# Both maxima of a pair of heads ahead of one joint exponent bias, in a blocked attention layer

## The chip, the cores and the metric

The kernel runs on one core of a Trainium2 chip. The metric is the device time of one execution in microseconds, the median of three runs. The engines are TensorE (PE; PEld is its weight load), VectorE (DVE), ScalarE (ACT), GpSimd (POOL) and SyncE (SP), which issues the DMAs.

## What is computed

x is 4 x 1024 x 1024 (batch, tokens, features). The layer is an attention block with a conditioned norm, followed by a causal depthwise convolution of four taps. Cut to what matters here:

```python
xn = rms_norm(x, g_norm) * (1 + scale) + shift      # scale, shift from cond @ W_emb + b_emb
q, k, v = split(xn @ W_qkv)                         # 16 heads of 64
q, k = rms_norm(q, g_q), rms_norm(k, g_k)
attn = softmax(q @ k.T * 64 ** -0.5)                # per head, 1024 x 1024
o = attn @ v
x = x + o + o @ W_out
out = x + causal_conv(x, cond) + b                  # taps from cond, four rows
```

The convolution's weights are the 4 x 1024 conditioning array, one row per tap. The softmax subtracts each row's maximum. A row is one query of one head; its maximum over 1024 keys is what the change is about.

## The kernel before, in words

**Units.** There are U = 32 units (4 batches x 8 pairs of heads, K = 8). Unit u does the attention of one pair of heads for all 1024 queries, in eight steps p = 0 to 7 of 128 queries each. So there are 256 steps, and each handles both heads h = 0, 1: slot s = 2p + h. Beside its attention a unit carries, spread by hand over its eight steps, the projection of unit u + 1 (`project`, L1016), head norms (`sums`, `normalise`), the input norm of x for the next batch (`x_multiply`, `x_shift`), and from unit 8 on the output product of the batch before (`out_product`, L1050) and its convolution (`convolve`, L1703 to L1714). Float32 accuracy comes from pairs of float16 halves, high and low, so most products are three matmuls.

**One step, engine by engine.** Each engine has its own program in a fixed order, and semaphores tie them.

- TensorE: `score(u, p)` (L958) waits until both exponents of step p - 1 are done (`exp_done` at slot 2p), since there is one PSUM tile `scores` [128, 2, 1024] for both heads. It issues 12 matmuls, the two heads alternating, so that both heads' scores are complete within the last two. Then come second halves of `attend` (L977), `inverses` (L992), `project` or `out_product`, first halves of `attend`, and the next `score`. How much lies between two scores differs by p: at p = 6 and 7 of a steady unit it is least.
- VectorE: `maximum(u, p, h)` (L1558) for h = 0 and 1: a tensor_reduce over 1024 scores gives minus the row maximum, and a tensor_scalar (L1561) turns it into the exponent's bias. After both come the unit's other vector work of that step, then `low(u, p, 0)` and `low(u, p, 1)` (L1567), which wait for the high halves, then in some steps more work (`x_multiply` at p = 0, `sums` at p = 3, `normalise` at p = 5).
- ScalarE: other work, then `exponent(u, p, 0)` and `(u, p, 1)` (L1201), each waiting for `bias_done` of its own slot; each also reads out the row sum. Then `read_inverses` at even p, `high(u, p, 0)` and `(u, p, 1)` (L1209, the float16 high half), and more.
- SyncE: `transpose_p` (L762) transposes each slot's probabilities by DMA once `lo_done` tells of its low half; `attend` reads them one or two steps later.

The exponent's input stays in PSUM, in `scores`, until it has run; `prob` (in the tile `late`) has one place for each of the two heads.

**Special units.** Units 1 to 6 also prepare a part of the projection of the unit after next (`gives_early`), units 1 to 7 prepare W_out (`wo_maximum`, `wo_lower`), and unit 31 is followed by a tail of output products. `keep_clock` issues matmuls whose result nobody reads.

Of the kernel before, what the change touches and what calls it, by code (L numbers as in the profile page):

```python
# [12 lines left out]
ALU = mybir.AluOpType  # L13
ACT = mybir.ActivationFunctionType
AX = mybir.AxisListType
# [9 lines left out]
P_SHIFT = 12 * float(np.log(2.0))  # L25
# [441 lines left out]
def main(nc, const, shared, w_dram, mod_dram, xn_dram, o_dram, x, W_qkv, W_out, out):  # L467
# [15 lines left out]
    with ExitStack() as ctx:  # L483
        def sb(name, shape, dt):
            return ctx.enter_context(nc.sbuf_tensor(name, shape, dt))

        def psum(name, shape, dt):
            return ctx.enter_context(nc.psum_tensor(name, shape, dt))

        def sem(name):  # L490
            return ctx.enter_context(nc.semaphore(name))
# [18 lines left out]
        neg = sb("neg", [P, NS], F32)  # L510
        bias = sb("bias", [P, NS], F32)
# [16 lines left out]
        scores = psum("scores", [P, 2, N], F32)  # L528
# [51 lines left out]
        qk_done = sem("qk_done")  # L580
        max_done = sem("max_done")
        bias_done = sem("bias_done")
# [107 lines left out]
        def slot(u, s):  # L690
            return NS * u + s

        def static(u):
            return isinstance(u, int)
# [856 lines left out]

        @block.vector
        def _(dve):
            def maximum(u, p, h):
                s = 2 * p + h
                n = slot(u, s)
                dve.wait_ge(qk_done, n + 1)
                nc.vector.tensor_reduce(neg[:, s:s + 1], scores[:, h, :], axis=AX.X, op=ALU.max,  # L1558
                                        negate=True).then_inc(max_done, 1)
                dve.wait_ge(max_done, n + 1)  # L1560
                nc.vector.tensor_scalar(bias[:, s:s + 1], neg[:, s:s + 1], const["l_scale"][:, 0:1], P_SHIFT,  # L1561
                                        ALU.mult, ALU.add).then_inc(bias_done, 1)

            def low(u, p, h):
                s = 2 * p + h
# [29 lines left out]
            def x_mean(v, i, ring):  # L1595
                dve.wait_ge(x_sq, v - K + 1)
                need(dve, x_pw, v - K - ring + 1)
                nc.vector.tensor_scalar(msx[:, i, 1:2], msx[:, i, 0:1], 1.0 / D, EPS, ALU.mult,
                                        ALU.add).then_inc(x_ms, 1)
# [13 lines left out]
            def x_shift(v, buffer):  # L1613
                dve.wait_ge(x_mul, v + 1)
                nc.vector.tensor_tensor(buffer, buffer, rows[:, 1], ALU.add).then_inc(x_mod, 1)
# [15 lines left out]
            def wo_maxima():  # L1631
                dve.wait_ge(wo_mx, K)
                nc.vector.tensor_reduce(wo_top[:, 0:1], wo_max[:], axis=AX.X, op=ALU.max).then_inc(wo_rows, 1)
# [29 lines left out]
            def invert(u, g, par):  # L1663
                n = NG * u + g
                dve.wait_ge(exp_done, slot(u, 4 * g) + 4)
                need(dve, inv_tr, n - 1)
                col = par * NS + 4 * g
                nc.vector.reciprocal(inv[:, g % 2, :], total[:, col:col + 4]).then_inc(inv_rc, 1)
                dve.wait_ge(inv_rc, n + 1)
                one_ = inv[:, g % 2, :].rearrange("p (a h) -> p a h", a=2)  # L1670
                nc.vector.tensor_scalar(inv_pair[:, g % 2, :, 0:2], one_, INV_UP, None, ALU.mult).then_inc(inv_hi, 1)
                dve.wait_ge(inv_hi, n + 1)
                nc.vector.scalar_tensor_tensor(out=inv_pair[:, g % 2, :, 2:4], in0=one_, scalar=INV_UP,
                                               in1=inv_pair[:, g % 2, :, 0:2], op0=ALU.mult,
                                               op1=ALU.subtract).then_inc(inv_done, 1)
# [15 lines left out]
            def convolve(T, par, hh, i):  # L1691
                n = 4 * T + 2 * hh + i
                m = 2 * hh + i
                c = 4 * par + m
                y_, acc_ = yT_of(T), acc_of(T)
                if T == U - 1 and m == 2:
                    dve.wait_ge(y_first, 1)
                else:
                    dve.wait_ge(y_ev, 2 * T + hh + 1)
                if T != U - K - 1:  # L1700
                    need(dve, *stored(T - (2 if static(T) and T >= U - K else 1), hh))
                need(dve, halo, 2 * n)
                nc.vector.tensor_scalar(y_[:, m, 0:H], ends[:, c, :], const["carry"][:, bass.ds(T, 1)], None,  # L1703
                                        ALU.mult).then_inc(halo, 1)
                for k in range(TAPS - 1, -1, -1):
                    if k == TAPS - 1:
                        nc.vector.tensor_scalar(acc_[:, m, :], y_[:, m, k:k + QG], const["taps"][:, k, c:c + 1],
                                                const["conv_b"][:, c:c + 1], ALU.mult, ALU.add).then_inc(cv, 1)
                        dve.wait_ge(halo, 2 * n + 1)
                        nc.vector.tensor_copy(ends[:, c, :], y_[:, m, QG:QG + H]).then_inc(halo, 1)  # L1710
                        dve.wait_ge(halo, 2 * n + 2)
                    else:
                        dve.wait_ge(cv, 4 * n + TAPS - 1 - k)
                        nc.vector.scalar_tensor_tensor(out=acc_[:, m, :], in0=y_[:, m, k:k + QG],  # L1714
                                                       scalar=const["taps"][:, k, c:c + 1], in1=acc_[:, m, :],
                                                       op0=ALU.mult, op1=ALU.add).then_inc(cv, 1)

            def unit(u, par, qkv, xs, outs, fins):
                w, v, T = u + 1, u + K, u - K
                begun = not (static(u) and u == 0)  # L1720
                last = u + 1 == U
                for p in range(K):
                    maximum(u, p, 0)
                    maximum(u, p, 1)
                    if p == 0:
                        if xs:
                            x_mean(v, par, 2)
                        if begun:
                            invert(u - 1, 3, 1 - par)
                    if p == 1:  # L1730
                        if fins:
                            convolve(T - 1, 1 - par, 0, 1)
                        if xs:
                            x_shift(v, x_in[:])
                    if p in (2, 4, 6):
                        invert(u, p // 2 - 1, par)
                    if p == 2:
                        if outs and par == 0:
                            set_scale(T)
                        if fins:  # L1740
                            convolve(T - 1, 1 - par, 1, 0)
                    if p == 3 and fins:
                        convolve(T - 1, 1 - par, 1, 1)
                    if p == 4 and qkv:
                        normalise(w, 0)
                    if p == 5 and qkv:
                        sums(w, 1)
                    if p == 6 and qkv and not outs:
                        normalise(w, 1)
                    if last and p == 5:  # L1750
                        set_scale(U - K)
                    if u in (1, 2) and p < 4:
                        wo_maximum(4 * u - 4 + p)
                    if u == 3 and p == 0:
                        wo_maxima()
                    if u == 3 and p == 2:
                        wo_scales()
                    if 4 <= u < K and p in (2, 4):
                        wo_lower(2 * u - 8 + p // 2 - 1)
                    if p == 7 and outs and not last:  # L1760
                        convolve(T, par, 0, 0)
                    elif p == 7 and qkv:
                        read_keys(w, 1 - par)
                    if p % 2 == 0 and p >= 4:
                        scale_values(u, (p - 4) // 2)
                    elif p % 2 == 0 and begun:
                        scale_values(u - 1, 2 + p // 2)
                    low(u, p, 0)
                    low(u, p, 1)
                    if p == 0 and xs:  # L1770
                        x_multiply(v, par, x_in[:])
                    if p == 3 and qkv:
                        sums(w, 0)
                    if p == 5 and qkv and outs:
                        normalise(w, 1)
# [89 lines left out]
```

## Time and profile before

| | us |
|---|---|
| median of 3 runs | 2477.79 |
| lowest and highest | 2477.67, 2483.67 |
| span of the profiled execution | 2476.2 |
| TensorE busy | 2362.7 |
| VectorE busy | 2089.6 |
| ScalarE busy | 1825.8 |
| GpSimd busy | 641.1 |

The profile is one execution of the program; its span runs from the first to the last instruction, and the device time of a run lies 1 to 2 us above such a span. Times are in us from the start of the span. Engines overlap, so busy times don't add up. Matmuls are pipelined, and their ends are modelled. In a timeline row the number behind the start is how long the row's instructions took together, xN how many there are, and brackets give the engine's idle time ahead of them and who ended it. In a chain of waits each step is followed back to what released it.

### The profile page before, as it was taken

Reading aid. Unit: us, or ns where it says so; the run is one execution under the profiler, and the core shown is the slowest. Engines: PE = TensorE matmul, PEld = TensorE weight load, DVE = VectorE, ACT = ScalarE, POOL = GpSimd, SP = SyncE. Lnnn points to the kernel's source line nnn. Section 1 sums busy time; section 2 is a strip of 40 time slices with the busy share of each in tenths; the row PEclk is TensorE's granted clock in tenths of the full one; section 3 lists DMA queues with packets and bytes.
Section 4 is the critical chain, followed back from the end, with each engine's and each line's share of the span. In section 5 each row is a group of like instructions: output and inputs, shape, how many; then the busy total and the mean of one; then the engine's idle time right before and its main releaser. Section 6 shows DMA issues by size and latency. Waiting matters only on the chain.

```text
span 2476.2 us, 54245 instructions
## 1 busy us (share of the span) xinstructions
PE 2362.7 (95%) x20794; PEld 1524.8 (62%) x20794; DVE 2089.6 (84%) x3368; ACT 1825.8 (74%) x2834; POOL 641.1 (26%) x451
## 2 busy tenths in 40 slices
PE   4799998999899999999999999999999999999899
PEld 0455555555466666666666666666666666666688
DVE  7769888888778888888888888888888888888876
ACT  5477778888777777877777787777777777777732
POOL 1132232332233222333332223233212222221100
PEclk9899999999999999999999999999999999999999
DMA  9999999999998989999999999999988888889971
GB/s 360 311 217 223 192 183 194 180 193 224 201 196 181 197 182 213 181 199 223 201 213 182 210 186 196 184 191 228 202 174 170 180 172 163 171 166 173 182 188 52
DMA packets 1234737, 484.99 MB, mean 196 GB/s; under 512 B 1139632, under 2 KB 1197872, under 8 KB 1232048
## 3 DMA queue, kind: packets, MB, share of 16 engines
q1 hardware_dynamic: 1234480, 481.53, 92.4%
q8 instruction: 166, 2.72, 0.5%
q14 instruction: 91, 0.75, 0.1%
HBM read 137.20 MB, written 56.66 MB: 78 GB/s over the span
## 4 chain that ended last, share of the span: by engine, by line
PE 64%; DVE 20%; issue 5%; ACT 4%; SPq 2%; DMA 1%; POOL 0%; ACTq 0%; POOLq 0%
PE proj L1016 33%; PE scores L958 10%; DVE neg L1558 9%; PE values L977 9%; PE proj L1050 8%; DVE p_pair L1567 7%; ACT p_pair L1209 3%; DVE bias L1561 2%; PE proj L1056 1%; PE misc L1068 1%; SPq L762 1%; ACT late L1201 1%; DMA w_sb<-w_dram 1%; PE values L992 1%; PE values L984 1%
## 5 line engine op out<-in xcount | busy, mean ns | idle before, releaser
L1016 PE MATMUL proj<-w_sb,xn_sb 128*128 128x384 f16 x6144 | 1035.2, 327 | 20.8 <-DMA w_sb<-w_dram 13.2
L1201 ACT ACTIVATE late<-scores,bias,l_scale 128x1024 f32<-128x1024 f32 x512 | 615.6, 1203 | 344.9 <-DVE bias L1561 325.8
L1016 PEld LDWEIGHTS proj<-w_sb,xn_sb 128*128 128x128 f16 x6144 | 587.2, 98 | 425.4 <-issue 25.9
L1567 DVE TENSOR_TENSOR p_pair<-late,p_pair 128x1024 f16<-128x1024 f32 x512 | 616.2, 1245 | 124.9 <-ACT p_pair L1209 124.8
L1558 DVE TENSOR_REDUCE neg<-scores 128x1 f32<-128x1024 f32 x512 | 623.0, 1217 | 107.0 <-PE scores L958 103.6
L1209 ACT ACTIVATE p_pair<-late 128x1024 f16<-128x1024 f32 x512 | 510.9, 1050 | 0.0
L977 PE MATMUL values<-pT,v_pair 128*64 128x256 f16 x6144 | 389.7, 277 | 14.6 <-ACT inv_row L1269 14.6
L958 PE MATMUL scores<-late 64*128 64x512 f16 x3072 | 376.1, 378 | 15.0 <-ACT late L1201 12.9
L977 PEld LDWEIGHTS values<-pT,v_pair 128*64 128x64 f16 x6144 | 319.0, 111 | 94.1 <-issue 70.3
L1474 POOL TENSOR_TENSOR rs<-ms,power 128x16 f32<-128x16 f32 x63 | 183.1, 2906 | 404.1 <-DVE ms L1581 403.7
L1050 PE MATMUL proj<-late,wo 128*128 128x256 f16 x2304 | 267.7, 273 | 1.3 <-issue 1.3
L1503 POOL TENSOR_TENSOR oT_pair<-oT,oT_pair 128x256 f16<-128x256 f32 x124 | 144.4, 1164 | 461.0 <-ACT oT_pair L1285 461.0
L958 PEld LDWEIGHTS scores<-late 64*128 64x128 f16 x3072 | 128.9, 94 | 195.7 <-issue 45.6
L1050 PEld LDWEIGHTS proj<-late,wo 128*128 128x128 f16 x2304 | 220.5, 98 | 31.5 <-issue 1.6
L1479 POOL TENSOR_TENSOR qk_pair<-stage,qk_pair 128x512 f16<-128x512 f32 x126 | 145.4, 1174 | 330.4 <-ACT qk_pair L1232 330.4
L1714 DVE SCALAR_TENSOR_TENSOR late<-late,taps 128x256 f32<-128x256 f32 x324 | 157.1, 485 | 11.6
L1217 ACT ACTIVATE stage<-proj 128x384 f32<-128x384 f32 x256 | 122.2, 477 | 29.8 <-PE proj L1016 29.8
L1269 ACT ACTIVATE inv_row<-values 4x256 f16<-4x256 f16 x128 | 46.9, 366 | 119.2 <-PE values L992 119.2
L1561 DVE TENSOR_SCALAR bias<-neg,l_scale 128x1 f32<-128x1 f32 x512 | 109.7, 214 | 18.1
L1499 POOL TENSOR_TENSOR pair<-x_in,pair 128x1024 f16<-128x1024 f32 x24 | 66.2, 2757 | 206.5 <-ACT pair L1263 199.5
L1201 ACT ACTIVATION_READ_ACCUMULATOR late<-scores,bias,l_scale 128x1 f32 x512 | 98.5, 192 | 0.0
L1050 PE MATMUL proj<-xn_sb,wo 128*128 128x256 f16 x744 | 86.5, 273 | 1.2 <-ACT late L1307 1.2
(183 smaller groups left out, 2023.6 us busy)
## 6 DMA issues: line engine op xcount, KB each, us to landing
w_sb<-w_dram SPq DMA_DIRECT2D x121, 384.0 KB, 4.1
o_dram<-oT_pair SPq DMA_DIRECT2D x124, 128.0 KB, 2.4
out<-late SPq DMA_DIRECT2D x54, 256.0 KB, 2.9
x_in<-in_x SPq DMA_DIRECT2D x25, 512.0 KB, 4.6
late<-in_x SPq DMA_DIRECT2D x25, 512.0 KB, 4.1
wq_raw<-in_L_cond_W_qkv SPq DMA_DIRECT2D x8, 1536.0 KB, 11.2
late<-o_dram SPq DMA_DIRECT2D x12, 1024.0 KB, 6.1
xn_dram<-late SPq DMA_DIRECT2D x21, 512.0 KB, 3.6
```

Source lines behind the costliest of these rows:

```text
L958: last = nc.tensor.matmul(scores[:, h, n * HN:(n + 1) * HN], stack[rows_, par, i, p * P:(p + 1) * P], stack[rows_, par, j, n * HN:(n + 1) ...
L977: last = nc.tensor.matmul(values[DH * h:DH * h + DH, 0:QG].rearrange("p (a n) -> p a n", a=2), v_pair[:, par, 2 * c + h, DH * i:DH * i + D ...
L1016: last = nc.tensor.matmul(proj[:, t % 2, 0:6 * DH], xn_sb[:, t, i * K + c, :], w_sb[:, c, j, :], start=(c == 0 and i == j == 0), stop=(c = ...
L1050: last = nc.tensor.matmul(dst, const["wo"][:, c, b, m * P:(m + 1) * P], oT_[:, c, a, :], start=(c == 0 and a == b == 0 and c1 == K), stop= ...
L1201: nc.scalar.activation(prob[:, h, :], scores[:, h, :], ACT.Exp, bias=bias[:, s:s + 1], scale=const["l_scale"][:, 0:1], accum_out=total[:, ...
L1209: nc.scalar.activation(p_pair[:, s % 4, 0, :], prob[:, h, :], ACT.Copy).then_inc(hi_done, 1)
L1474: nc.gpsimd.tensor_tensor(rs[:], ms[:], const["power"][:, 0:4 * KH], ALU.pow).then_inc(h_pw, 1)
L1479: last = nc.gpsimd.tensor_tensor(qk_pair[:, j, 1].rearrange("p t (h d) -> p (t h) d", d=DH), stage[:, hf, :, j * DH:(j + 1) * DH], qk_pair ...
L1558: nc.vector.tensor_reduce(neg[:, s:s + 1], scores[:, h, :], axis=AX.X, op=ALU.max, negate=True).then_inc(max_done, 1)
L1561: nc.vector.tensor_scalar(bias[:, s:s + 1], neg[:, s:s + 1], const["l_scale"][:, 0:1], P_SHIFT, ALU.mult, ALU.add).then_inc(bias_done, 1)
L1567: nc.vector.tensor_tensor(p_pair[:, s % 4, 1, :], prob[:, h, :], p_pair[:, s % 4, 0, :], ALU.subtract).then_inc(lo_done, 1)
L1714: nc.vector.scalar_tensor_tensor(out=acc_[:, m, :], in0=y_[:, m, k:k + QG], scalar=const["taps"][:, k, c:c + 1], in1=acc_[:, m, :], op0=AL ...
```

## The change

`maximum(u, p, h)`, called for h = 0 and then h = 1, becomes `maxima(u, p)`. It issues both tensor_reduces, each behind the wait for its own head's scores, then waits for both and makes the two biases with one tensor_scalar over two columns, which raises `bias_done` by two. Nothing on the other engines changes: `exponent` still waits for its own slot's count.

```diff
--- before.py
+++ after.py
@@ -1551,15 +1551,16 @@
 
         @block.vector
         def _(dve):
-            def maximum(u, p, h):
-                s = 2 * p + h
-                n = slot(u, s)
-                dve.wait_ge(qk_done, n + 1)
-                nc.vector.tensor_reduce(neg[:, s:s + 1], scores[:, h, :], axis=AX.X, op=ALU.max,
-                                        negate=True).then_inc(max_done, 1)
-                dve.wait_ge(max_done, n + 1)
-                nc.vector.tensor_scalar(bias[:, s:s + 1], neg[:, s:s + 1], const["l_scale"][:, 0:1], P_SHIFT,
-                                        ALU.mult, ALU.add).then_inc(bias_done, 1)
+            def maxima(u, p):
+                n = slot(u, 2 * p)
+                for h in range(2):
+                    s = 2 * p + h
+                    dve.wait_ge(qk_done, n + h + 1)
+                    nc.vector.tensor_reduce(neg[:, s:s + 1], scores[:, h, :], axis=AX.X, op=ALU.max,
+                                            negate=True).then_inc(max_done, 1)
+                dve.wait_ge(max_done, n + 2)
+                nc.vector.tensor_scalar(bias[:, 2 * p:2 * p + 2], neg[:, 2 * p:2 * p + 2], const["l_scale"][:, 0:1],
+                                        P_SHIFT, ALU.mult, ALU.add).then_inc(bias_done, 2)
 
             def low(u, p, h):
                 s = 2 * p + h
@@ -1720,8 +1721,7 @@
                 begun = not (static(u) and u == 0)
                 last = u + 1 == U
                 for p in range(K):
-                    maximum(u, p, 0)
-                    maximum(u, p, 1)
+                    maxima(u, p)
                     if p == 0:
                         if xs:
                             x_mean(v, par, 2)
```

## Rows read from the trace of the kernel before

**Rows 1.** The page, busy time, share of the span and instructions of each engine.

```profile
PE 2362.7 (95%) x20794; PEld 1524.8 (62%) x20794; DVE 2089.6 (84%) x3368; ACT 1825.8 (74%) x2834; POOL 641.1 (26%) x451
```

**Rows 2.** The page, the chain that ended last, shares by engine.

```profile
PE 64%; DVE 20%; issue 5%; ACT 4%; SPq 2%; DMA 1%; POOL 0%; ACTq 0%; POOLq 0%
```

**Rows 3.** Stretches: start:end, length, busy (instructions) by engine, granted clock, DMA share, GB/s.

```profile
core 0: us, PE busy (x) PEld busy (x) DVE busy (x) ACT busy (x) POOL busy (x), PEclk, DMA share, GB/s
398.50:594.90 196.40, 182.00 (x1576) 107.54 (x1576) 167.61 (x236) 163.73 (x254) 60.27 (x42) 0.97 0.97 195
...
664.60:2308.20 1643.60, 1642.21 (x14806) 1077.15 (x14804) 1415.29 (x2261) 1266.06 (x1988) 454.92 (x308) 1.00 0.94 190
2308.20:2361.80 53.60, 44.03 (x455) 31.82 (x455) 45.54 (x79) 37.75 (x59) 3.92 (x3) 1.00 1.02 197
```

**Rows 4.** Waits over the whole span: us in total, times, longest us.

```profile
ACT late L1201 <- DVE bias L1561: 325.8, 216, 6.9
...
DVE p_pair L1567 <- ACT p_pair L1209: 124.8, 172, 2.3
```

**Rows 5.** Timeline of VectorE, from unit 15's p = 7 to unit 16's p = 5.

```profile
1231.78 1.22 DVE L1558 TENSOR_REDUCE neg<-scores 128x1 f32<-128x1024 f32 x1
1233.03 0.21 DVE L1561 TENSOR_SCALAR bias<-neg,l_scale 128x1 f32<-128x1 f32 x1
1233.16 1.21 DVE L1558 TENSOR_REDUCE neg<-scores 128x1 f32<-128x1024 f32 x1
1234.41 0.21 DVE L1561 TENSOR_SCALAR bias<-neg,l_scale 128x1 f32<-128x1 f32 x1
1234.54 0.22 DVE L1703 TENSOR_SCALAR late<-ends,carry 128x3 f32<-128x3 f32 x1
...
1236.93 2.36 DVE L1567 TENSOR_TENSOR p_pair<-late,p_pair 128x1024 f16<-128x1024 f32 x2 [0.22 <-ACT p_pair L1209]
1239.21 1.22 DVE L1558 TENSOR_REDUCE neg<-scores 128x1 f32<-128x1024 f32 x1
...
1285.43 1.23 DVE L1558 TENSOR_REDUCE neg<-scores 128x1 f32<-128x1024 f32 x1 [1.64 <-PE scores L958]
```

**Rows 6.** Timeline of ScalarE, the exponents of four steps in the same units.

```profile
1228.06 0.19 ACT L1201 ACTIVATION_READ_ACCUMULATOR late<-scores,bias,l_scale 128x1 f32 x1
...
1233.28 1.20 ACT L1201 ACTIVATE late<-scores,bias,l_scale 128x1024 f32<-128x1024 f32 x1 [1.21 <-DVE bias L1561]
...
1234.66 1.21 ACT L1201 ACTIVATE late<-scores,bias,l_scale 128x1024 f32<-128x1024 f32 x1
1235.76 0.19 ACT L1201 ACTIVATION_READ_ACCUMULATOR late<-scores,bias,l_scale 128x1 f32 x1
...
1243.19 0.19 ACT L1201 ACTIVATION_READ_ACCUMULATOR late<-scores,bias,l_scale 128x1 f32 x1
...
1287.85 1.20 ACT L1201 ACTIVATE late<-scores,bias,l_scale 128x1024 f32<-128x1024 f32 x1
...
1289.04 1.21 ACT L1201 ACTIVATE late<-scores,bias,l_scale 128x1024 f32<-128x1024 f32 x1
```

**Rows 7.** Groups by line: busy us, mean ns of one, idle before and releaser.

```profile
L1567 DVE TENSOR_TENSOR p_pair<-late,p_pair 128x1024 f16<-128x1024 f32 x512 | 616.2, 1245 | 124.9 <-ACT p_pair L1209 124.8
...
L1561 DVE TENSOR_SCALAR bias<-neg,l_scale 128x1 f32<-128x1 f32 x512 | 109.7, 214 | 18.1
...
L1581 DVE TENSOR_SCALAR ms<-ms,eps_u 128x16 f32<-128x16 f32 x63 | 15.4, 245 | 2.3
```

**Rows 8.** Timeline of TensorE, scores of units 15, 16 and 17.

```profile
1228.78 1.47 PE L958 MATMUL scores<-late 64*128 64x512 f16 x12
...
1236.01 1.47 PE L958 MATMUL scores<-late 64*128 64x512 f16 x12
...
1245.98 1.47 PE L958 MATMUL scores<-late 64*128 64x512 f16 x12
...
1307.55 1.47 PE L958 MATMUL scores<-late 64*128 64x512 f16 x12
```

**Rows 9.** Timeline of VectorE, unit 5: the lows of p = 3.

```profile
494.49 2.36 DVE L1567 TENSOR_TENSOR p_pair<-late,p_pair 128x1024 f16<-128x1024 f32 x2 [2.31 <-ACT p_pair L1209]
```

## The prediction, made before the changed kernel ran

> **What bounds the kernel now.** I read the busy shares first [rows 1]: TensorE is busy 95% of the span, VectorE 84%. Then the chain that ended last [rows 2]: 64% of it is TensorE, 20% VectorE, so the array is not the only limit. The table by stage [rows 3] says where each holds. Between 664.6 and 2308.2 us (units 8 to 30) TensorE is busy 1642 of 1644 us. In units 4 to 6 it is not (182 of 196 us), nor in the last unit (44 of 54 us). There something else sets the pace. The list of waits [rows 4] names it: ScalarE's exponents wait 326 us for the bias, and VectorE's lows (L1567) wait 125 us for ScalarE's highs.
>
> So two loops compete for each pair of heads. One is TensorE's own work. The other is the latency loop: maximum, bias, exponent, high half (ScalarE), low half (VectorE), next maximum. They meet at `score`, which needs both exponents of the pair before (one PSUM tile of scores for both heads).
>
> **The latency loop, from one pair.** Unit 15, p = 7 [rows 5, 6]: the first maximum starts at 1231.78, its bias at 1233.03 (1.25 later), the second maximum at 1233.16 (0.13 behind the bias's start), the second bias 1.25 after that. The exponents start at 1233.28 and 1234.66, 1.50 and 2.88 after the first maximum (0.25 after each bias started). The lows start at 1236.93, 5.15 after it, behind an idle 0.22: VectorE waits there for ScalarE. The next maximum is at 1239.21, 2.28 behind the lows and with no idle ahead of it.
>
> **The change, costed on the same pair.** Removed: one [128,1] tensor_scalar per pair, 256 of 512 at 214 ns [rows 7], 55 us of busy time. Moved: the first bias behind the second maximum. Added: a wait of the joint bias for the second maximum, with everything behind it on VectorE queued and the first exponent on ScalarE waiting.
> The trace has no two maxima back to back. Two lows are: they take 2.36 together and 1.245 alone, so the second starts some 1.12 after the first [rows 5, 7]; a dependent step behind a maximum starts 1.25 after it. The second maximum is therefore 1.12 to 1.25 behind the first; I take 1.13, because the lows are the nearest case (same size, no dependence). The bias on two columns I price at one column's 0.21: a 128x16 tensor_scalar takes 245 ns [rows 7], so the error is at most 0.03.
> New times behind the first maximum: second maximum 1.13, bias 2.38, first exponent 2.63 (was 1.50). Second exponent: when both biases are already there, exponents start 1.19 apart (1287.85 and 1289.04 [rows 6]), so 3.82 (was 2.88). **The pair's end moves by +0.94** (bounds 0.93 and 1.09: the second maximum 0.01 earlier, or 0.12 later with a bias 0.03 longer), and the highs and lows with it. In return VectorE is free for its other work at 2.51 instead of 2.76 (1234.54 [rows 5]), **0.25 earlier**. That gain counts only where VectorE reaches its lows after the highs are done.
>
> By the Trainium skill (VectorE: DVE Perf Modes, Rules for kernel authors) one should minimise the count of vector instructions; by it this change would gain. The same skill (Perfetto Trace Analysis, Optimizing Scalar/DVE Operations) limits that: grouping helps a saturated engine, and where the engine is not saturated but causes bubbles elsewhere, broken-up instructions may finish work sooner. The idle ahead of the lows agrees with the second.
>
> **Steady units (9 to 30, 71.54 us each: scores at 1236.01 and 1307.55 [rows 8]).** I carry the delay from pair to pair, against TensorE's own lag. At p = 1 to 6 TensorE reaches the scores at least 2.5 us after the exponents ended (p = 1: 1245.98 against 1243.38 [rows 6, 8]), so 0.94, even added up over the loop, doesn't stop it there. VectorE's idle ahead of the maxima of p = 3 and p = 5 (1.64 [rows 5]) absorbs what has built up: p = 3 starts level with TensorE's lag, p = 3 and 4 add 0.94 each, and 1.88 - 1.64 leaves some 0.25 at p = 5. There the exponents were held by ScalarE's own work (2.42 behind the maximum [rows 5, 6], now 2.63), so +0.21 only. Then the tight place, where TensorE's pieces between scores are short:
> - p = 6: maximum 0.25 + 0.21 less 0.07 of idle = 0.39 late, exponents 0.39 + 0.94 = 1.33 late. TensorE had 0.53 behind the exponent's end (1228.25 to 1228.78 [rows 6, 8]), of which 0.06 is the signal; so the scores of p = 7 come 1.33 - 0.47 = 0.86 late.
> - p = 7: the lows of p = 6 are ACT-bound, the maximum follows them at once: 1.33 late; exponents 2.27 late. TensorE had no margin here (exponent ends 1235.95, scores 1236.01). So the scores of the next p = 0 are 2.27 late, and TensorE has lost it.
> The same accounts for unit 8. 23 units x 2.27 = **52 us**.
>
> **Early units.** In units 3 to 6 VectorE never idles before a maximum: the latency loop itself is the period. Unit 5: its lows wait for ScalarE by 0.4 to 2.3 us at six of eight pairs (2.31 at p = 3 [rows 9]); at p = 6 both arrive together; only at p = 4 is VectorE itself late (normalise and wo_lower lie before its lows, and it doesn't idle). Seven pairs give +0.94 and p = 4 gives -0.25: +6.3 for the unit. The same sum gives 6.3 and 6.1 for units 4 and 6, 7.3 for unit 3 (its p = 4 has no wo_lower). Units 0, 1, 2 and 7 have pairs that TensorE or a load starts, which absorb part: I get 3.7, 5.7, 5.9 and 4.0. Sum **45 us**. The last unit is again all latency loop: TensorE is idle for 10 of its 54 us [rows 3]. Pairs 0 to 6 set the scores of p = 7, behind which the tail starts: six times 0.94 and once 0.66 (p = 2, where VectorE had reached its lows 0.28 after ScalarE): **6 us**. The tail has none of this.
>
> **Clock.** In units 4 to 6 the granted clock is 0.97, against 1.00 in the steady ones [rows 3]: short stretches at 1.2 in place of 2.4 GHz, behind idle of the array. 0.97 over 196 us is 12 us at half speed, three units' worth, so some 4 us at half speed (2 us of array time) per unit. More idle may add one such stretch per unit; the array is then mostly not the limit, so I take a quarter: 8 units x 0.5 = 4 us (0 to 16 in the range).
>
> **Sum.** 52 + 45 + 6 + 4 = 107 us. The profiled execution's span is 2476.2 against a median of 2477.8 for the runs, so 107 on the median: **2585 us**, 4.3% slower.
>
> **Rivals.**
> - VectorE's throughput is the bound, so less work on it wins: 256 x 0.25 = 64 us faster, 2414. For it: 84% busy, and at 3 of 8 steady pairs (p = 1, 2, 4) no idle ahead of the lows. Against it: idle ahead of most lows, and TensorE's 1642 of 1644 us, which no saving on VectorE shortens. It would decide if VectorE's own work between maxima and lows were over 0.94 us longer than the way through ScalarE at p = 6 and 7; at p = 7 it is 0.22 shorter. Chance 0.03.
> - TensorE's stored-up work covers the delay: within 0.3% (7 us, about what a measurement of this kernel can tell from no change). For it: 2.5 us of margin at most pairs. Against it: 0.47 and 0 at p = 7 and p = 0. Chance 0.04.
> - Only the seam costs: p = 7 to p = 0 alone, with the loop's delay not carried from pair to pair. 31 seams x 0.94 = 29 us, 2507; anything from 2485 to 2548 counts here. Chance 0.06.
> - The margins are used up everywhere and each pair pays: 256 x 0.94 = 241 us, 2718; or idle drops the clock in most units. Over 2620: chance 0.07.
> - My walk in its range: 0.80.
>
> **Range.** Low: a steady unit at 1.8 (no carry from p = 3 and 4, which takes 0.25, and 0.2 of error in the margins), 23 x 1.8 = 41, early units at two thirds, 30: about 71, 2548. High: +1.09 instead of +0.94 makes 103 into 119, clock 16, the rest for margins that I took as too wide: 2620. **2548 to 2620** leaves out 0.06 + 0.07 + 0.07 = 0.20. Faster 0.03, same 0.04, slower 0.93.
>
> **What would show it.** Maxima 1.1 to 1.25 apart, first exponent 2.6 behind the first maximum; the exponents' wait for the bias clearly above 326 us; VectorE's lows waiting for ScalarE well above 125 us; TensorE waiting at the scores of p = 7 and p = 0 in every steady unit, some 0.8 and 1.4 us; unit period near 73.8; unit 5 near 71 instead of 64.6. I am wrong if the steady period stays at 71.5, if the maxima don't overlap as the lows do, or if the tight pairs show the new time on another queue.

## The result, and the profile after

The changed kernel takes 2633.97 us (median of 4 runs, 2630.93 to 2636.45) against 2479.74 us (4 runs) for the kernel before: ratio 1.0622, interval 1.061 to 1.0635. It is 154 us, 6.2%, slower. The forecast had the sign and the place of most of the loss, but 107 us; the result lies above its range. The profiled execution took 2636.45 us, its span is 2634.5, 158 more than before; sums over the trace below are made against 158, sums over medians against 154.

The page of the changed kernel: busy time, shares of the chain that ended last, and the groups that answer to [rows 1, 2, 4, 7]. The line numbers of VectorE's steps are one higher (maximum L1559, bias L1562, low L1568).

```profile
PE 2389.2 (91%) x20794; PEld 1530.0 (58%) x20794; DVE 2068.5 (79%) x3112; ACT 1796.4 (68%) x2834; POOL 646.5 (25%) x451
...
DVE 45%; PE 22%; issue 17%; ACT 11%; DMA 1%; POOL 1%; SPq 1%; ACTq 0%; DVEq 0%; POOLq 0%
...
L1201 ACT ACTIVATE late<-scores,bias,l_scale 128x1024 f32<-128x1024 f32 x512 | 611.8, 1199 | 629.7 <-DVE bias L1562 629.7
...
L1568 DVE TENSOR_TENSOR p_pair<-late,p_pair 128x1024 f16<-128x1024 f32 x512 | 604.8, 1223 | 276.0 <-ACT p_pair L1209 276.0
...
L958 PE MATMUL scores<-late 64*128 64x512 f16 x3072 | 388.7, 387 | 141.4 <-ACT late L1201 140.9
...
L1562 DVE TENSOR_SCALAR bias<-neg,l_scale 128x2 f32<-128x2 f32 x256 | 91.8, 359 | 27.8 <-DVE neg L1559 0.5
```

VectorE did drop 256 instructions and 21 us of busy time. In return ScalarE waits 630 us for the bias instead of 326, the lows wait 276 us for ScalarE instead of 125, and TensorE's scores now wait 141 us for the exponents. TensorE's share of the last chain fell from 64% to 22%: most of the kernel is now set by the latency loop. And one mean is off: a joint bias takes 359 ns, where I had priced it at 210.

The same stretch as the long one of [rows 3], units 8 to 30, in the changed kernel:

```profile
core 0: us, PE busy (x) PEld busy (x) DVE busy (x) ACT busy (x) POOL busy (x), PEclk, DMA share, GB/s
...
719.40:2457.40 1738.00, 1652.99 (x14806) 1081.63 (x14807) 1399.27 (x2078) 1247.61 (x1990) 461.31 (x308) 1.00 0.88 179
```

It is 1738.0 us long instead of 1643.6, and TensorE is idle for 85 us of it instead of 1.4. Of the 158 us, 94.4 arise here, 54.8 had arisen before it (664.6 against 719.4), and 9 arise in the last unit and the tail.

The timelines of the tight place, unit 15's p = 6 and p = 7, answer to [rows 5, 6, 8]. VectorE:

```profile
1310.44 2.35 DVE L1559 TENSOR_REDUCE neg<-scores 128x1 f32<-128x1024 f32 x2
1312.89 1.18 DVE L1562 TENSOR_SCALAR bias<-neg,l_scale 128x2 f32<-128x2 f32 x1
...
1317.84 2.36 DVE L1568 TENSOR_TENSOR p_pair<-late,p_pair 128x1024 f16<-128x1024 f32 x2 [0.52 <-ACT p_pair L1209]
1320.12 2.35 DVE L1559 TENSOR_REDUCE neg<-scores 128x1 f32<-128x1024 f32 x2
1322.57 0.23 DVE L1562 TENSOR_SCALAR bias<-neg,l_scale 128x2 f32<-128x2 f32 x1
...
1326.30 2.36 DVE L1568 TENSOR_TENSOR p_pair<-late,p_pair 128x1024 f16<-128x1024 f32 x2 [1.40 <-ACT p_pair L1209]
```

GpSimd, ScalarE and TensorE beside it:

```profile
1311.78 2.27 POOL L1479 TENSOR_TENSOR qk_pair<-stage,qk_pair 128x512 f16<-128x512 f32 x2 [4.25 <-ACT qk_pair L1232]
```

```profile
1314.11 1.20 ACT L1201 ACTIVATE late<-scores,bias,l_scale 128x1024 f32<-128x1024 f32 x1 [2.41 <-DVE bias L1562]
...
1322.84 1.20 ACT L1201 ACTIVATE late<-scores,bias,l_scale 128x1024 f32<-128x1024 f32 x1 [2.63 <-DVE bias L1562]
```

```profile
1316.65 1.47 PE L958 MATMUL scores<-late 64*128 64x512 f16 x12 [1.78 <-ACT late L1201]
...
1325.37 1.47 PE L958 MATMUL scores<-late 64*128 64x512 f16 x12 [1.56 <-ACT late L1201]
```

At p = 7 the pair runs nearly as forecast: the bias starts 2.45 behind the first maximum (forecast 2.38), the first exponent 2.72 behind it (2.63), against 1.50 before; the second follows 1.20 later, 3.92 instead of 2.88. The difference, +1.03 over many pairs, I call the pair's extra time; forecast was 0.94. At p = 6 the picture is another: the bias lasts 1.18 us, and the first exponent starts 3.67 behind the first maximum. GpSimd runs its two L1479 from 1311.78 to 1314.05; the second of them starts within 0.01 of the bias, and the bias ends at 1314.07, 0.02 behind it. TensorE then stalls at the scores of p = 7 and of the next p = 0, where the forecast put its stalls, but by 1.78 and 1.56 us, not 0.8 and 1.4.

The instructions of the bias line alone, duration in ns (least/median/most):

```profile
L1562 DVE TENSOR_SCALAR bias<-neg,l_scale x256: 227/228/1190, 141.2 to 2523.3; 128x2 f32<-128x2 f32 x128
```

47 of the 256 take over 0.3 us, 43 us together: 23 of them at p = 6 of units 8 to 30 (about 1.18 each), 12 at p = 5 of the even units among these (0.57), the others at p = 7 of the early units (0.43 to 0.90) and at p = 2 of units 4 to 7 (0.77). Each of the 47 ends within 0.03 us of the end of a GpSimd subtraction (L1479, L1488 or L1499). Not every GpSimd instruction does this: 30 biases lie wholly inside the 2.9 us of the power L1474 and take their 0.23, as at p = 4 of unit 15:

```profile
1291.51 2.91 POOL L1474 TENSOR_TENSOR rs<-ms,power 128x16 f32<-128x16 f32 x1 [10.55 <-DVE ms L1582]
```

```profile
1293.79 0.23 DVE L1562 TENSOR_SCALAR bias<-neg,l_scale 128x2 f32<-128x2 f32 x1
```

### The profile page after: what moved, and what is told of

It is laid out like the page before. It is cut to its first block, busy times and chain, and to the rows that moved or that the text cites. A ratio compares the mean times of both kernels' runs of the same rounds, so it can differ in the third digit from the quotient of the medians.

```text
span 2634.5 us, 54245 instructions
## 1 busy us (share of the span) xinstructions
PE 2389.2 (91%) x20794; PEld 1530.0 (58%) x20794; DVE 2068.5 (79%) x3112; ACT 1796.4 (68%) x2834; POOL 646.5 (25%) x451
## 4 chain that ended last, share of the span: by engine, by line
DVE 45%; PE 22%; issue 17%; ACT 11%; DMA 1%; POOL 1%; SPq 1%; ACTq 0%; DVEq 0%; POOLq 0%
DVE neg L1559 18%; DVE p_pair L1568 17%; PE proj L1016 10%; ACT p_pair L1209 7%; PE scores L958 4%; ACT late L1201 4%; PE values L977 3%; PE proj L1050 3%; DVE bias L1562 3%; DVE x_in L1611 1%; DVE ms L1579 1%; DVE stage L1590 1%; DVE late L1715 1%; PE misc L1068 1%; DVE stage L1594 1%
## 5 line engine op out<-in xcount | busy, mean ns | idle before, releaser
L1568 DVE TENSOR_TENSOR p_pair<-late,p_pair 128x1024 f16<-128x1024 f32 x512 | 604.8, 1223 | 276.0 <-ACT p_pair L1209 276.0
L1559 DVE TENSOR_REDUCE neg<-scores 128x1 f32<-128x1024 f32 x512 | 601.1, 1215 | 32.3 <-PE scores L958 32.3
L958 PE MATMUL scores<-late 64*128 64x512 f16 x3072 | 388.7, 387 | 141.4 <-ACT late L1201 140.9
L1503 POOL TENSOR_TENSOR oT_pair<-oT,oT_pair 128x256 f16<-128x256 f32 x124 | 161.1, 1299 | 568.6 <-ACT oT_pair L1285 568.6
L1474 POOL TENSOR_TENSOR rs<-ms,power 128x16 f32<-128x16 f32 x63 | 183.0, 2905 | 361.2 <-DVE ms L1582 357.8
L1479 POOL TENSOR_TENSOR qk_pair<-stage,qk_pair 128x512 f16<-128x512 f32 x126 | 144.7, 1169 | 372.0 <-ACT qk_pair L1232 372.0
L1715 DVE SCALAR_TENSOR_TENSOR late<-late,taps 128x256 f32<-128x256 f32 x324 | 157.0, 485 | 11.6
L1683 DVE TENSOR_TENSOR oT<-values,inv_all 128x256 f32<-128x256 f32 x128 | 54.3, 424 | 133.9 <-ACT inv_all L1275 133.9
L1562 DVE TENSOR_SCALAR bias<-neg,l_scale 128x2 f32<-128x2 f32 x256 | 91.8, 359 | 27.8 <-DVE neg L1559 0.5
L1499 POOL TENSOR_TENSOR pair<-x_in,pair 128x1024 f16<-128x1024 f32 x24 | 55.8, 2327 | 228.2 <-ACT pair L1263 221.4
```

The source lines that it names most:

```text
L958: last = nc.tensor.matmul(scores[:, h, n * HN:(n + 1) * HN], stack[rows_, par, i, p * P:(p + 1) * P], stack[rows_, par, j, n * HN:(n + 1) ...
L1474: nc.gpsimd.tensor_tensor(rs[:], ms[:], const["power"][:, 0:4 * KH], ALU.pow).then_inc(h_pw, 1)
L1503: nc.gpsimd.tensor_tensor(o_half(u, g, 1), oT[:], o_half(u, g, 0), ALU.subtract).then_inc(o_low, 1)
L1562: nc.vector.tensor_scalar(bias[:, 2 * p:2 * p + 2], neg[:, 2 * p:2 * p + 2], const["l_scale"][:, 0:1], P_SHIFT, ALU.mult, ALU.add).then_in ...
L1568: nc.vector.tensor_tensor(p_pair[:, s % 4, 1, :], prob[:, h, :], p_pair[:, s % 4, 0, :], ALU.subtract).then_inc(lo_done, 1)
```

## The experiments

Each is the kernel before, or the changed kernel, with one edit, shortened here where dots stand. Each was timed beside the kernel before on the same chip, and its loss is counted from the median of that kernel there (2476.68, 2478.14 or 2478.48).

**Order alone.** The changed kernel with both maxima first, then two one-column biases, each of which waits for its own maximum only.

```diff
-dve.wait_ge(max_done, n + 2)
-nc.vector.tensor_scalar(bias[:, 2 * p:2 * p + 2], neg[:, 2 * p:2 * p + 2], ...).then_inc(bias_done, 2)
+for h in range(2):
+    s = 2 * p + h
+    dve.wait_ge(max_done, n + h + 1)
+    nc.vector.tensor_scalar(bias[:, s:s + 1], neg[:, s:s + 1], ...).then_inc(bias_done, 1)
```

> The change with both maxima first, but with two biases of one column each behind them. In the changed kernel 47 of the 256 two-column biases take 0.27 to 1.19 us in place of 0.23, 33 us in all, each while GpSimd is at work; 23 of them stand at p = 6 of the steady units, on the way to the scores of p = 7. Theory A (the order costs some 1.0 us per pair at the tight places, and the joint bias of two columns waits for GpSimd on top): no bias over 0.3 us, and 115 to 130 us over the kernel before instead of 154. Theory B (the order is all, and any bias that stands behind both maxima runs into the same delay): 145 to 155 us over, with long biases at p = 6 again.

Measured: 2565.6 us, ratio 1.036 (1.0345 to 1.0376), +89 us. The exponents start 2.50 and 3.70 behind the first maximum, so the pair's extra time is 0.82. No bias is long:

```profile
L1564 DVE TENSOR_SCALAR bias<-neg,l_scale x512: 196/206/216, 138.8 to 2452.9; 128x1 f32<-128x1 f32 x171
```

Even the order alone costs more than half of it, with the instruction count unchanged; but it is less than I expected, and 65 us of the 154 need something else.

**Two columns alone.** The kernel before in its old order, each bias made two columns wide (the second a constant that nobody reads), 512 of them. `neg` and `bias` are twice as long for it, and the maxima and exponents use every second column.

```diff
-nc.vector.tensor_scalar(bias[:, s:s + 1], neg[:, s:s + 1], ...
+nc.vector.tensor_scalar(bias[:, 2 * s:2 * s + 2], neg[:, 2 * s:2 * s + 2], ...
```

> The kernel before, in its own order, but each bias computes two columns: its own and a second one that holds a constant and that nobody reads (each slot has two columns in neg and bias). The work on the way is the same but for the width. Theory A: the first or second bias of p = 6 in steady units waits for GpSimd by about 1 us, as those of p = 7 in early units, and the kernel is 20 to 35 us slower than before. Theory B (order alone): within 8 us of before.

Measured: 2528.07 us, ratio 1.0205 (1.0186 to 1.0225), +51 us for the width alone. The group's mean rises from 214 to 382 ns, and 113 of the 512 take over 0.3 us. The timeline of unit 15 shows two of these at p = 6 and a short one at p = 7:

```profile
L1561 DVE TENSOR_SCALAR bias<-neg,l_scale 128x2 f32<-128x2 f32 x512 | 195.4, 382 | 18.1
```

```profile
1254.10 1.23 DVE L1558 TENSOR_REDUCE neg<-scores 128x1 f32<-128x1024 f32 x1
1255.36 1.11 DVE L1561 TENSOR_SCALAR bias<-neg,l_scale 128x2 f32<-128x2 f32 x1
1256.39 1.21 DVE L1558 TENSOR_REDUCE neg<-scores 128x1 f32<-128x1024 f32 x1
1257.63 1.07 DVE L1561 TENSOR_SCALAR bias<-neg,l_scale 128x2 f32<-128x2 f32 x1
...
1263.57 1.22 DVE L1558 TENSOR_REDUCE neg<-scores 128x1 f32<-128x1024 f32 x1
1264.82 0.23 DVE L1561 TENSOR_SCALAR bias<-neg,l_scale 128x2 f32<-128x2 f32 x1
```

A maximum is never lengthened (1.21 to 1.23 in every run); a bias of two columns is, from 0.23 to 1.1. The 51 us are more than the 20 to 35 expected. In 28 pairs both biases are caught, as in the rows above, and 38 of the 113 long ones lie in units 0 to 7, where this kernel loses 20 us; how the 51 us divide between these was not tested.

**Waiting alone.** VectorE as before; only the first exponent waits until both biases are there.

```diff
-act.wait_ge(bias_done, slot(u, s) + 1)
+act.wait_ge(bias_done, slot(u, 2 * p) + 2)
```

> The kernel before, VectorE untouched, but each pair's first exponent waits for both biases. First exponent 2.88 behind the first maximum (was 1.50), second 4.07 (was 2.88), so the pair's end is 1.19 later, against 1.03 in the changed kernel, and no bias has two columns. If the later exponents are what costs, this alone gives 125 to 150 us over before, with idle on TensorE ahead of the scores of p = 7 and p = 0. If instead VectorE's two maxima back to back or the joint bias were at fault, it stays below 40 us.

Measured: 2635.95 us, ratio 1.0638 (1.0622 to 1.0655), +159 us: about as much as the whole change, without touching VectorE. The exponents start 2.88 and 4.08 behind the first maximum, an extra of 1.19 per pair. That the exponents start later is sufficient to cost this much, whatever VectorE does or saves. That the two totals nearly agree is chance: this kernel delays each pair by more (1.19 against 1.03) and has no lengthened bias.

```profile
L1201 ACT ACTIVATE late<-scores,bias,l_scale 128x1024 f32<-128x1024 f32 x512 | 611.9, 1199 | 639.6 <-DVE bias L1561 638.9
```

**GpSimd out of the way at p = 6.** The changed kernel, with GpSimd's work of p = 6 (both L1479, and L1488 behind them) held back until the joint bias of p = 6 is done.

```diff
 if p == 6 and qkv:
+    pool.wait_ge(bias_done, slot(u, 12) + 2)
     half_low(w, 1)
```

> The changed kernel, but GpSimd begins half_low(w, 1) at p = 6 only when the joint bias of p = 6 is made, so the two can't overlap there; VectorE is untouched. Theory A: the biases of p = 6 are back at 0.23 us, 23 units x 0.95 us come back, 130 to 136 us over before. TensorE reads half_low's result some 2.8 us after it is ready, so the later GpSimd work should cost nothing. Theory B (the length of that bias has another cause): the biases of p = 6 stay long and the time at 154.

Measured: 2612.97 us, ratio 1.0551 (1.0536 to 1.0567), +136 us, at the upper end of what was expected: 18 given back by the 136 against 154, 21 by the two medians. Between unit 8 and unit 31 the trace loses 72.3 us instead of 94.4. GpSimd's L1479 beside it is therefore what lengthens the bias of p = 6, and that is worth 18 to 22 us. The bias line now has 906 ns as its longest: the waits of the other pairs are still there.

**Where the time is lost.** Two kernels split the change by place: the changed kernel with the old order at p = 6 and 7 of units 8 on, and the kernel before with the joint bias there alone.

```diff
+if u >= K and p >= 6:          # the second kernel: if u < K or p < 6
+    maximum(u, p, 0)
+    maximum(u, p, 1)
+else:
+    maxima(u, p)
```

> The changed kernel, but in units 8 to 31 the pairs p = 6 and p = 7 keep the old order with one-column biases. If the steady units lose at the seam (p = 6 to p = 0), where TensorE has least between two scores, then they lose only what the carried delay of p = 5 (0.65 us) and the new stall at p = 1 (0.86 us, units 9 to 23) give: 80 to 95 us over before. If every pair pays alike, 8 to 31 lose 6/8 of their 100 us: about 130 us over.

> The mirror of that: the kernel before, with the joint bias only at p = 6 and p = 7 of units 8 to 31. Seam theory: a steady unit loses 2.9 us (exponents of p = 6 2.0 late against a margin of 0.47, those of p = 7 1.03 more), 23 x 2.9 + 1 = 65 to 75 us over before. Every pair alike: 2/8 of 100, so 25 us.

Measured: 2563.47 us, ratio 1.0343 (1.0325 to 1.0361), +85 us; and 2546.77 us, ratio 1.0274 (1.0253 to 1.0295), +69 us. Both as expected, and together 154, the whole. A quarter of the pairs in units 8 to 31, two of eight, is worth 69 us.

**The stall at p = 1.** The trace of the changed kernel has a stall that the forecast lacks. At p = 1 of units 9 to 23 TensorE waits before the transposes L1068 for VectorE's convolution (L1715), which lies behind the maxima of p = 1 and is late with them. In the kernel before it doesn't wait there.

```profile
1343.74 0.66 PE L1068 MATMUL misc<-eye,late 128*128 128x128 f32 x4 [0.76 <-DVE late L1715]
```

The changed kernel with these transposes moved behind the values product of that step:

```diff
-if fins and p == 1 and not last:
-    out_transposes(T - 1, 0, (k_ev, u + 1))
 ...
 elif p == 1 and begun:
     attend(u - 1, 3, 1 - par, 0)
-if last and p == 1:
+if fins and p == 1:
     out_transposes(T - 1, 0, (k_ev, u + 1))
```

> The changed kernel, but at p = 1 TensorE issues the transposes of the convolved rows behind the first half of attend and no longer ahead of it. In the changed kernel it waits there 0.77 us for VectorE's convolution, which starts 1.0 us late behind the late maximum of p = 1; the units 9 to 23 lose 0.86 us each at p = 1. If that is this wait, it goes, and 10 to 14 us come back: 140 to 144 us over before. If the loss at p = 1 is another wait: still 154.

Measured: 2624.19 us, ratio 1.0589 (1.057 to 1.0607), 8 to 10 us given back, by the 146 against 154 or by the two medians, a little less than the 10 to 14 expected. By the trace the loss from the scores of p = 1 to those of p = 2 falls from 0.86 to 0.03 us in units 9 to 23, 12.5 us in all, and rises from nothing to 0.15 in units 24 to 30, 1 us. The losses at p = 6 and p = 7 stay as they were.

**A way to gain?** Where the loop is the period, something else may be moved off it. In the kernel before, the step `wo_lower` of p = 4 in units 4 to 7 lies ahead of late lows; I moved it to p = 5.

```diff
-if 4 <= u < K and p in (2, 4):
-    wo_lower(2 * u - 8 + p // 2 - 1)
+if 4 <= u < K and p in (2, 5):
+    wo_lower(2 * u - 8 + p // 4)
```

> The kernel before, with the wo_lower of p = 4 in units 4 to 7 moved to p = 5. In these units VectorE reaches the lows of p = 4 late (6.64 us behind the maximum against 5.43 through ScalarE), and TensorE waits for the exponents at p = 5; at p = 5 VectorE idles 0.9 us ahead of its lows, in which 0.9 of the 1.28 us fit. If the early units are paced by this loop, each gains 0.8 us: 2 to 4 us faster, 0.1%. If TensorE's own order paces them: no difference.

Measured over 12 runs: 2478.42 against 2478.14 us, ratio 1.0 (0.999 to 1.001); no difference, so the gain of 2 to 4 us didn't come. The lows of p = 4 do start 5.45 behind the maximum instead of 6.64, and those of p = 5 5.59 instead of 5.15, as expected. In the one trace of this kernel units 4, 6 and 7 are 0.6 to 1.0 us shorter, no more than such units differ between traces where the edit doesn't touch them (up to 1.5 us in the second seam kernel). Unit 5 is 3.3 us longer, and there TensorE's projection waits 2.99 us for its weights, where it was 1.43 before. Whether that wait follows from the edit wasn't tested.

```profile
514.16 6.94 PE L1016 MATMUL proj<-w_sb,xn_sb 128*128 128x384 f16 x24 [2.99 <-DMA w_sb<-w_dram]
```

**Order and wait, one column each.** The last open term: the changed kernel with its wait for both maxima, but two one-column biases behind it. All that the forecast priced is in it; what is left out is what makes the bias joint, its second column and its increment of `bias_done` by two.

```diff
 dve.wait_ge(max_done, n + 2)
-nc.vector.tensor_scalar(bias[:, 2 * p:2 * p + 2], neg[:, 2 * p:2 * p + 2], ...).then_inc(bias_done, 2)
+for h in range(2):
+    s = 2 * p + h
+    nc.vector.tensor_scalar(bias[:, s:s + 1], neg[:, s:s + 1], ...).then_inc(bias_done, 1)
```

> The changed kernel with its wait for both maxima, but the joint bias split into two biases of one column each. It tells the width of the bias from the wait: with the split and each bias waiting for its own maximum alone, the first exponent started 2.50 behind the first maximum (89 us over before), in the changed kernel 2.72 and far later where GpSimd works (154 us). Theory A: the 0.22 us come from the wait for the second maximum, so the first exponent is at 2.72 again in every pair, no bias is longer than 0.3 us, a steady unit loses 2 x 1.03 plus a carry of some 0.3 at the seam and 0.86 at p = 1, and the kernel is 120 to 130 us over before. Theory B: the 0.22 us come from the second column, so the time is that of the other split, 85 to 95 us over.

Measured: 2587.55 us, ratio 1.0437 (1.0418 to 1.0455), +109 us, between the two outcomes that were expected. The exponents start 2.63 and 3.83 behind the first maximum, an extra of 0.95.

```profile
L1564 DVE TENSOR_SCALAR bias<-neg,l_scale x512: 202/210/216, 139.7 to 2473.8; 128x1 f32<-128x1 f32 x171
```

In the changed kernel the first exponent starts 0.09 later than here, and most of that is not the second column. The bias itself starts later there, 2.45 behind the first maximum against 2.38; from its start to the exponent it is 0.264 against 0.249. In the kernel with two columns in the old order the bias starts as before (1.25 behind its maximum), and from it to the exponent it is 0.264 too. So the width accounts for 0.015, and the 0.07 came with the joint instruction. Its wait for the maxima is an instruction of its own in the trace, which neither the one-column kernels nor the old order with two columns has:

```profile
L1561 DVEq EVENT_SEMAPHORE  x256: 21/21/21, 141.2 to 2523.2; - x128
```

Whether this separate wait is what costs the 0.07 wasn't isolated.

So the 154 us come apart like this, each step a measured kernel: order alone 89; waiting for the other maximum too, 0.13 us a pair, 109 - 89 = 20; the joint bias in place of two single ones, 154 - 109 = 45. The last can be split with one interpolation: from an extra of 0.95 to one of 1.19 (the kernel that only waits) the loss rises by 50 us, so the 0.08 by which the pair ends later, 1.03 against 0.95, would be 50 x 0.08 / 0.24 = 17. That leaves 28 for the biases that GpSimd lengthens, of which 18 to 22 are measured at p = 6. The 17 and 28 are an estimate; the 45 and the 18 to 22 are not.

## Why the prediction was right in sign and too small

What the forecast took as its terms, beside the kernel that has all of them but the joint bias, and the changed kernel (us, rounded, from the starts of the scores in the traces):

| stretch | forecast | order and wait, one column | changed kernel |
|---|---|---|---|
| units 0 to 7, with the clock | 45 + 4 | 42 | 55 |
| units 8 to 30 | 52 | 58 | 94 |
| last unit and tail | 6 | 8 | 9 |
| sum | 107 | 109 | 158 |

**Right.** The maxima are 1.13 apart, as taken from the lows. The first exponent at 2.63 is what the one-column kernel shows to the hundredth. TensorE is caught at p = 7 and at p = 0, and the early units lose over their whole length. The first rival, VectorE's own work as the bound, falls: 21 us less of its work, 154 us lost, and the same loss without touching it. The second, that stored-up work covers the delay, falls with TensorE's 141 us of waiting at the scores. Seam only with no carry (29 us) falls against 69 us for the seam of the steady units alone and 85 us with that seam spared. The fourth, over 2620, names the measured time, but its mechanism isn't what happened: in units 9 to 30 nothing is lost between the scores of p = 2 and those of p = 6, and the loss of such a unit, 3.4 to 4.6 us, arises behind the scores of p = 6, p = 7 and p = 1 alone.

**Wrong: "The bias on two columns I price at one column's 0.21 [...] so the error is at most 0.03."** This step failed, and it cost the 45 us between 109 and 154. The bias of two columns is lengthened by GpSimd's subtractions, where the one-column bias isn't: 0.95 more at p = 6 in 23 steady units, 22 us by the trace, and 0.34 at p = 5 in the 12 even ones, where the maximum of p = 6 then comes 0.65 late and not 0.35. And in every undisturbed pair the first exponent starts 0.09 later than priced (2.72 against 2.63), 0.07 of it because the joint bias starts later. I leaned on a mean, 245 ns for a 128x16 tensor_scalar. The trace of the kernel before held the counter-evidence beside it. By instruction, in that trace:

```profile
L1671 DVE TENSOR_SCALAR inv_pair<-inv x128: 169/169/1143, 156.6 to 2372.9; 128x4 f16<-128x4 f32 x128
...
L1581 DVE TENSOR_SCALAR ms<-ms,eps_u x63: 233/234/469, 116.0 to 2290.1; 128x16 f32<-128x16 f32 x63
```

A step of four columns with 169 ns as its median took up to 1143. And right behind the bias of p = 6 in unit 15, the pair ahead of the one that I costed, such steps wait and the bias doesn't, still in the kernel before:

```profile
1226.70 0.21 DVE L1561 TENSOR_SCALAR bias<-neg,l_scale 128x1 f32<-128x1 f32 x1
...
1227.04 0.51 DVE L1671 TENSOR_SCALAR inv_pair<-inv 128x4 f16<-128x4 f32 x1
1227.58 1.07 DVE L1673 SCALAR_TENSOR_TENSOR inv_pair<-inv,inv_pair 128x4 f16<-128x4 f32 x1
```

```profile
1225.25 2.27 POOL L1479 TENSOR_TENSOR qk_pair<-stage,qk_pair 128x512 f16<-128x512 f32 x2 [4.12 <-ACT qk_pair L1232]
1227.48 1.15 POOL L1488 TENSOR_TENSOR v_pair<-stage,v_pair 128x512 f16<-128x512 f32 x1
```

L1671 ends at 1227.55 and L1479 at 1227.52; L1673 ends at 1228.65 and L1488 at 1228.63. The bias of one column, in the middle of L1479, takes its 0.21. The Trainium skill (SBUF — State Buffer, Who interferes with whom) has the rule: VectorE and GpSimd share a pair of ports as an exclusive lock, whoever starts first holds the other up, and a tensor_scalar takes part in it only in its two-port mode, a tensor_reduce never. The traces agree in part: biases of two columns up to 1190 ns in the changed kernel, of one never over 217 in any run, maxima never longer. They don't show the rest: the second L1479 starts within 0.01 us of the bias that it outlasts, so who was first can't be read, and the power L1474, which runs 2.9 us, holds up none of the 30 biases inside it; there the measurement decides. That the lock is the mechanism is the skill's statement; the runs show a dependence on the width and on which GpSimd instruction runs beside it, and only the widths one and two were compared in the same place.

**Wrong, smaller, and partly cancelling.** The forecast asked at p = 1 to 6 only whether TensorE reaches its scores in time, and not its other waits for VectorE. The transposes at p = 1 cost 0.86 x 15 = 13 us in the changed kernel, and 0.82 a unit in the one-column one. Against that, what is carried into p = 6 from the earlier pairs was taken as 0.39 and is about 0.1 in the one-column kernel: its late steady units (24 on) lose 2.0, where twice 0.95 and 0.1 are 2.0 and the forecast had 2.27. In the early units the sum was 49 for 42. One reading there was wrong: VectorE does idle before a maximum in units 3 to 6, once, for 1.40 us at p = 7 of unit 6. With both, an extra of 0.95 gave the forecast's total nearly exactly, in part by these errors' balance. The clock had its small term: from the first scores to unit 31 the trace of the changed kernel shows about twice the time at 1.2 GHz (some 57 us against 27), which wasn't isolated and lies within the table's numbers.

## What to carry to other kernels

- Merging two small operations makes the first consumer wait for the last producer. On a loop of latency that costs more than an instruction saves: here 1.0 to 1.2 us later exponents for one instruction of 0.21 us. If the order must be changed, let each operation wait for its own producer only; that alone was 20 us.
- Price an operation that changes its width not by the mean of a similar one but by its longest, and look at what the other engine does when it is long: about half of the joint bias's cost sat in one place of eight, beside a GpSimd instruction that already lengthened its neighbours.
- When a delay is walked through a bottleneck engine, check each wait that this engine has for the delayed one, not only the one at which the loop closes.

## What was not expected of the hardware

Four things. A tensor_scalar on one column (128x1) takes 212 to 216 ns in the kernel before, though GpSimd runs at 207 of its 512 starts, 147 of them outside of L1474; on two columns it takes 228 ns alone and up to 1190 beside a GpSimd subtraction, or up to 1973 in the kernel with two columns in the old order. Beside GpSimd's power on 128x16 (L1474) two columns take 228 ns as well. A bias that waits for the second maximum starts the exponents 0.13 us later than one that waits for the first, even though both stand behind the second maximum on VectorE (2.63 against 2.50). And delays of VectorE and ScalarE cost more than in proportion: an extra of 0.82, 0.95 and 1.19 us a pair gave 89, 109 and 159 us, that is 108, 115 and 134 us for each us of delay, more the longer the delay. In the late steady units (24 on) TensorE's margin of 0.47 behind p = 6 is seen to be used up: the loss from the scores of p = 6 to those of p = 7 is 0.34, 0.57 and 1.37 us.
